# Gathered features per block from 16, 16, 16, 16 to 16, 15, 15, 15, with another way of comparing ids in the first block

## Chip, cores and metric

The kernel runs on one core of a Trainium2 chip. The metric is the device time of one execution in microseconds (us), the median of the runs shown; less is better.

## What is computed

A recommendation tower: for each of 2,048 samples 26 table rows are looked up by id, the 27 vectors (dense features and 26 rows) are multiplied with each other, and the 351 products go through three dense layers together with the dense features.

```
e = jnp.stack([tbl_0[ids[:, 0]], ..., tbl_25[ids[:, 25]]], axis=1)     # [2048, 26, 128]
combined = jnp.concatenate([dense_features[:, None, :], e], axis=1)    # [2048, 27, 128]
interactions = jnp.einsum('bfd,bgd->bfg', combined, combined)
z = jnp.concatenate([dense_features, interactions[:, _IU0, _IU1]], axis=1)   # upper triangle, 351
h = jnp.concatenate([z, dense_features], axis=1)                        # 607 columns
h = jnp.maximum(h @ W_top1 + b_top1, 0.0)      # 607 x 512
h = jnp.maximum(h @ W_top2 + b_top2, 0.0)      # 512 x 256
y = h @ W_top3                                  # 256 x 1
```

Four tables have 12,500 or 125,000 rows, the others 1,000 or 1,250.

## The kernel before

The samples are cut into 16 tiles of 128, four tiles to a block of 512. A table row reaches its sample in one of two ways.

- **Gathered** (`gather`, L676 to L682, on GpSimd's queue): per tile and feature one indirect DMA brings 128 rows to `rows`, which has room for two tiles. TensorE transposes them (`turn_group`, L806) in four groups of four features into PSUM; VectorE copies the even groups to `all_combined` (L1044), ScalarE the odd ones (L916).
- **Looked up** (`look_up`, L727): for a whole block and one feature TensorE multiplies the table, in chunks of 125 rows, with a one-hot matrix of 125 x 512 per chunk. A table of 1,000 rows has 8 chunks, one of 1,250 has 10. Each table is split in a high part (ScalarE's cast, L852) and a low part (VectorE's subtraction, "split", L1019), so each chunk is two matmuls. The one-hot matrices are made in halves of a look-up (4 or 5 chunks): by VectorE with one compare of ids against `row_bank`, row numbers that lie in PSUM (L1031), or, for the second half of the look-ups in `ACT_HOTS`, by ScalarE in two passes (L863, L870). `one_hot` holds 20 chunks. ScalarE copies the result out of PSUM (`copy_look`, L878) and later moves the looked-up columns of a tile to `all_combined` (`move_looks`, L897).

In every block the first 16 features of `SLOT_FEATURES` are gathered and the other 10 looked up. The looked-up features run forwards in even blocks and backwards in odd ones, so that a block's first four look-ups find their tables still in SBUF (`AGAIN`).

Per tile, TensorE multiplies the 27 vectors of four samples at a time (`dot_tile`, L821, four PSUM banks per tile, "dots"), ScalarE copies the banks (L925), and SP stores them to DRAM and loads them back as rows of pairs. The layers (L757, L766, L771, L783) of a block run during the next block ("products"); those of the last block run at the end in three pieces, with the exact fp32 product instead of three partial ones.

The order on TensorE is written out: the start (`START`) has all look-ups of block 0, with tile 0's transposes after the fourth; then per tile `dot_tile(t)` and `STEPS[t]`: the transposes of tile t+1, then `HALVES_AFTER` halves of look-ups for the next block, merged with products of the block before. VectorE keeps four halves ahead of it.

GpSimd's gathers for tile t+2 are let go in four steps:

```
pool.wait_ge(turned_done, groups_by(t))
gather(t + ROW_TILES, range(1))
for g in range(1, n_groups(t + ROW_TILES) - 1):
    if 0 < t <= LAST * PER_BLOCK:
        pool.wait_ge(half_done, halves_beside(t, g))
    gather(t + ROW_TILES, range(g, g + 1))
pool.wait_ge(dots_done, (t + 1) * FILLS - 1)
gather(t + ROW_TILES, range(n_groups(t + ROW_TILES) - 1, n_groups(t + ROW_TILES)))
```

So the last group of tile t+2 waits for the third bank of tile t's dots. SP's queue loads ids (`load_ids`, one row spread over all partitions, `ID_PLACES` look-ups of them), tables, weights, and carries the products' way through DRAM.

## Time and profile before

| what | value |
|---|---|
| timed runs, median (lowest to highest) | 379.48 us (379.36 to 380.45) |
| profiled execution, span (its own time is given as this span) | 496.1 us |
| PE, DVE, ACT, POOL busy in the span | 76%, 49%, 39%, 51% |
| instructions in the profile | 8,109 |
| DMA moved | 58.44 MB |

Engines: PE is TensorE (PEld its weight loads), DVE VectorE, ACT ScalarE, POOL GpSimd, SP the engine that issues most DMAs. A matmul in full fp32 leaves two records, one in fp32r leaves one: 64 matmuls of a tile's dots are 128 records. "issue" after a row means that the engine stood idle before it and waited for nothing that the profile shows; "remote" is a releaser that the profile does not know. The profiled execution is 116.6 us longer than the median of the timed ones.

### The profile page before, as it was taken

What the parts mean: (1) busy time and instruction counts of PE and PEld (TensorE: products, weight loads), DVE (VectorE), ACT (ScalarE), POOL (GpSimd) and SP (SyncE); (2) the same over time, 40 slices, a digit from 0 to 9 for tenths busy, and PEclk for the clock granted to TensorE, in tenths of its full rate; (3) what the DMA queues carried; (4) which work ended last, traced back from release to release, by engine and by line L of the source; (5) the groups of instructions that cost most, each with busy time, mean ns of one, the idle gap of its engine ahead of it and who ended that gap; (6) DMA issues with size and microseconds to landing.
All of it is one profiled execution on the core that took longest, in us unless ns stands there. A gap on an engine that the chain in (4) does not pass through costs nothing.

```text
span 496.1 us, 8109 instructions
## 1 busy us (share of the span) xinstructions
PE 376.0 (76%) x3360; PEld 301.4 (61%) x3360; DVE 244.4 (49%) x174; ACT 195.0 (39%) x261; POOL 254.8 (51%) x266
## 2 busy tenths in 40 slices
PE   1951777858586665978798796969788696879997
PEld 1630656647474554767586666867676455666787
DVE  4740789674919370765725750956566101112133
ACT  3810986414242521525252532434354334344400
POOL 6774540655737363646666554747466564730000
PEclk9985799989989796989998898989899898789899
DMA  8841763259915153456714533536232621123330
GB/s 210 218 134 41 218 187 85 70 156 275 227 29 161 45 155 103 109 150 153 183 46 128 160 87 104 143 93 193 74 89 63 168 73 27 49 63 100 69 71 5
DMA packets 38479, 58.44 MB, mean 118 GB/s; under 512 B 21665, under 2 KB 22561, under 8 KB 38444
## 3 DMA queue, kind: packets, MB, share of 16 engines
q1 hardware_dynamic: 29304, 40.74, 30.3%
q0 software_dynamic: 8192, 16.79, 13.5%
q8 instruction: 26, 0.43, 0.4%
q10 hardware_dynamic: 948, 0.41, 0.4%
q14 instruction: 9, 0.07, 0.0%
HBM read 47.68 MB, written 10.23 MB: 117 GB/s over the span
## 4 chain that ended last, share of the span: by engine, by line
PE 58%; issue 16%; DVE 11%; another core or an unknown queue 8%; SPq 3%; DMA 2%; ACT 2%; DVEq 0%; ACTq 0%
PE look_bank L727 25%; PE short_bank L821 15%; DVE one_hot L1031 8%; PE out_bank L757 6%; PE out_bank L771 4%; PE short_bank L806 4%; PE out_bank L766 3%; SPq L632 2%; DVE all_combined L1044 1%; DVE low_table L1019 1%; DMA spread_ids<-in_ids_by_feature 1%; PE out_bank L783 1%; SPq L621 1%; DMA last_scratch<-all_dots 1%
## 5 line engine op out<-in xcount | busy, mean ns | idle before, releaser
L682 POOL DMA_INDIRECT rows<-in_tbl,all_ids x256 | 253.9, 992 | 191.9 <-PE short_bank L821 81.9
L1031 DVE TENSOR_TENSOR one_hot<-spread_ids,row_bank 128x2048 fp32r<-128x2048 int32 (+3 forms) x80 | 170.7, 2175 | 27.1 <-PE look_bank L727 10.7
L727 PE MATMUL look_bank<-one_hot,high_table 125*128 125x512 f32 x328 | 140.8, 429 | 20.0 <-issue 16.1
L727 PE MATMUL look_bank<-one_hot,low_table 125*128 125x512 f32 x328 | 132.4, 404 | 0.6 <-issue 0.6
L821 PE MATMUL short_bank<-all_combined 128*59 128x54 f32 x2048 | 88.1, 247 | 53.2 <-issue 51.5
L821 PEld LDWEIGHTS short_bank<-all_combined 128*59 128x59 f32 x2048 | 79.7, 162 | 66.7 <-issue 66.5
L1044 DVE COPY all_combined<-short_bank 128x512 f32<-128x512 f32 x32 | 21.8, 691 | 156.2 <-PE short_bank L806 122.3
L727 PEld LDWEIGHTS look_bank<-one_hot,high_table 125*128 125x128 f32 x328 | 64.5, 197 | 40.5 <-issue 23.6
L727 PEld LDWEIGHTS look_bank<-one_hot,low_table 125*128 125x128 f32 x328 | 64.6, 197 | 16.9 <-issue 4.1
L925 ACT COPY all_dots<-short_bank 128x432 f32<-128x432 f32 x64 | 33.1, 518 | 97.1 <-remote 53.7
L878 ACT COPY looked_up<-look_bank 128x512 f32<-128x512 f32 x40 | 23.4, 586 | 120.8 <-remote 45.3
L806 PE MATMUL short_bank<-identity,rows 128*128 128x128 f32 x256 | 40.0, 290 | 38.7 <-issue 22.5
L806 PEld LDWEIGHTS short_bank<-identity,rows 128*128 128x128 f32 x256 | 28.9, 146 | 47.0 <-issue 27.0
L1019 DVE TENSOR_TENSOR low_table<-whole_table,high_table 125x1024 fp32r<-125x1024 f32 (+1 forms) x28 | 34.8, 1243 | 33.5 <-ACT high_table L852 22.7
L897 ACT COPY all_combined<-looked_up 128x1280 f32<-128x1280 f32 (+2 forms) x20 | 39.7, 1985 | 0.2
L852 ACT CAST high_table<-whole_table 125x1024 fp32r<-125x1024 f32 (+1 forms) x28 | 29.7, 1065 | 7.7 <-DMA whole_table<-in_tbl 7.7
L771 PE MATMUL out_bank<-hidden,w 128*128 128x512 f32 (+2 forms) x96 | 32.4, 470 | 0.0
L938 ACT ACTIVATE hidden<-out_bank,bias 128x512 f32<-128x512 f32 x18 | 15.4, 858 | 33.2 <-PE out_bank L757 18.3
L916 ACT COPY all_combined<-short_bank 128x512 f32<-128x512 f32 x32 | 19.9, 674 | 8.4 <-PE short_bank L806 8.4
L771 PEld LDWEIGHTS out_bank<-hidden,w 128*128 128x128 f32 x96 | 16.8, 199 | 6.3 <-issue 4.3
L1053 DVE TENSOR_SCALAR hidden<-out_bank,bias 128x128 f32<-128x128 f32 (+1 forms) x18 | 7.9, 437 | 22.2 <-PE out_bank L766 17.9
L863 ACT ACTIVATE one_hot<-spread_ids,chunk_row 128x512 fp32r<-128x512 int32 x24 | 15.4, 714 | 0.0
(42 smaller groups left out, 183.5 us busy)
## 6 DMA issues: line engine op xcount, KB each, us to landing
whole_table<-in_tbl SPq DMA_DIRECT2D x26, 448.0 KB
spread_ids<-in_ids_by_feature SPq DMA_DIRECT2D x40, 256.0 KB
block_scratch<-all_dots SPq DMA_DIRECT2D x24, 208.0 KB
rows<-in_tbl,all_ids POOLq DMA_INDIRECT x256
block_scratch<-all_dots SPq DMA_DIRECT2D x24, 104.0 KB
pairs<-block_scratch SPq DMA_DIRECT2D x72, 29.2 KB
whole_table<-in_tbl SPq DMA_DIRECT2D x26, 52.0 KB
whole_table<-in_tbl SPq DMA_DIRECT2D x2, 560.0 KB
```

Of the source, the lines that this page charges most:

```text
L682: nc.gpsimd.indirect_dma_start(rows[:, t % ROW_TILES, slot, :], None, tables[SLOT_FEATURES[slot]][:, :], bass.IndirectOffsetOnAxis(ap=all_ ...
L727: last = nc.tensor.matmul(look_bank[s % LOOK_BANKS][:], table_parts[part][TABLE_PLACE[s]][0:ROWS_K, c, :], one_hot[0:ROWS_K, (chunks_befor ...
L757: last = nc.tensor.matmul(out, w1_parts[weight][0:rows_k, k, i * P:(i + 1) * P], of_parts[of], start=(k == 0 and weight == of), stop=(k == ...
L771: last = nc.tensor.matmul(out, w2[:, k, o * P:(o + 1) * P], hidden1[:, k, a:b], start=(k == 0), stop=(k == last_k))
L806: last = nc.tensor.transpose(turn_bank(t, g)[:, q * P:(q + 1) * P], rows[:, t % ROW_TILES, slot, :], identity[:])
L821: last = nc.tensor.matmul(fill_bank(t, b)[row:row + LOADED, q * SQUARE:(q + 1) * SQUARE], all_combined[:, at:at + LOADED], all_combined[:, ...
L852: nc.scalar.copy(high_table[i][0:ROWS_K, 0:c, :], whole_table[i][0:ROWS_K, 0:c, :]).then_inc(table_high, 1)
L897: nc.scalar.copy(combined[:, :, 1 + GATHERED[m] + slot:1 + GATHERED[m] + slot + b - a], looked_up[:, place:place + b - a, u * P:(u + 1) * ...
L925: nc.scalar.copy(dots_of(h)[:, :, at:at + PER_BANK], fill_bank(t, b)[:, 0:PER_BANK * SQUARE].rearrange("p (q c) -> p c q", q=PER_BANK)).th ...
L1019: nc.vector.tensor_tensor(low_table[i][0:ROWS_K, 0:c, :], whole_table[i][0:ROWS_K, 0:c, :], high_table[i][0:ROWS_K, 0:c, :], ALU.subtract) ...
L1031: last = nc.vector.tensor_tensor(one_hot[:, place:place + n, :], spread_ids[:, s % ID_PLACES:s % ID_PLACES + 1, :].to_broadcast([P, n, COLS]),
L1044: nc.vector.tensor_copy(to, of).then_inc(even_copied, 1)
```

## The change

Blocks 1 to 3 gather 15 features and look up 11; the added one is feature 21, whose table has 1,250 rows. Their last group of transposes has three features. The numbers of halves per tile become 6, 5, 5, 6. `looked_up` has 16 places for 15, with a general search for the block that used a place before; `spread_ids` has 6 for 7. In block 0 (`s < FIRST_LOOK[1]`) VectorE compares one chunk per instruction, with the row number as an operand per partition from `chunk_row` in SBUF; in later blocks it compares as before. ScalarE makes 4 halves of block 0 (look-ups 1, 3, 5, 7) where it made 6 (1, 2, 4, 5, 7, 8).

```diff
-GATHERED = [16, 16, 16, 16]
+GATHERED = [16, 15, 15, 15]
...
-ID_PLACES = 7
-LOOK_PLACES = 15
+ID_PLACES = 6
+LOOK_PLACES = 16
...
-GROUPS = [[4, 4, 4, 4] for _ in range(BLOCKS)]
+GROUPS = [[4] * (n // 4) + [n % 4] * (n % 4 > 0) for n in GATHERED]
...
-HALVES_AFTER = [[6, 5, 5, 4] for _ in range(LAST)]
+HALVES_AFTER = [[6, 5, 5, 6], [6, 5, 5, 6], [6, 5, 5, 6]]
...
-ACT_HOTS = [1, 2, 4, 5, 7, 8]
+ACT_HOTS = [1, 3, 5, 7]
...
-    return BLOCK_OF[s] % 2 * (LOOK_PLACES - IN_BLOCK[0]) + LOOK_SLOT[s]
+    return BLOCK_OF[s] % 2 * (LOOK_PLACES - IN_BLOCK[BLOCK_OF[s]]) + LOOK_SLOT[s]
+
+
+def block_before(s):
+
+    earlier = [BLOCK_OF[i] for i in range(s) if look_place(i) == look_place(s)]
+    return earlier[-1] if earlier else None
...
             def copy_look(s):
-                if s >= LOOK_PLACES:
-
-                    act.wait_ge(look_moved, moves_by(BLOCK_OF[s - LOOK_PLACES] * PER_BLOCK + PER_BLOCK - 1))
+                if block_before(s) is not None:
+
+                    act.wait_ge(look_moved, moves_by(block_before(s) * PER_BLOCK + PER_BLOCK - 1))
...
-                for c, n, place in runs_of(s, h):
+                if s < FIRST_LOOK[1]:
+
+                    for c in halves(s)[h]:
+                        last = nc.vector.tensor_scalar(
+                            one_hot[:, (chunks_before(s) + c) % HOT_PLACES, :], spread_ids[:, s % ID_PLACES, :],
+                            chunk_row[CHUNKS[s]][:, c:c + 1], None, ALU.is_equal)
+                for c, n, place in runs_of(s, h) if s >= FIRST_LOOK[1] else []:
```

VectorE in the start, from its first half on, before (names: output, then inputs; partitions x elements, and the number of equal instructions in a row):

```order
L1031 TENSOR_TENSOR one_hot<-spread_ids,row_bank 128x2048
L1019 TENSOR_TENSOR low_table<-whole_table,high_table 125x1024
L1031 TENSOR_TENSOR one_hot<-spread_ids,row_bank 128x2048 x2
L1019 TENSOR_TENSOR low_table<-whole_table,high_table 125x1024
L1031 TENSOR_TENSOR one_hot<-spread_ids,row_bank 128x2048
L1019 TENSOR_TENSOR low_table<-whole_table,high_table 125x1024
L1031 TENSOR_TENSOR one_hot<-spread_ids,row_bank 128x2048
L1019 TENSOR_TENSOR low_table<-whole_table,high_table 125x1024
```

and the same place in the changed kernel:

```order
L1039 TENSOR_SCALAR one_hot<-spread_ids,chunk_row 128x512 x4
L1025 TENSOR_TENSOR low_table<-whole_table,high_table 125x1024
L1039 TENSOR_SCALAR one_hot<-spread_ids,chunk_row 128x512 x8
L1025 TENSOR_TENSOR low_table<-whole_table,high_table 125x1024
L1039 TENSOR_SCALAR one_hot<-spread_ids,chunk_row 128x512 x4
L1025 TENSOR_TENSOR low_table<-whole_table,high_table 125x1024
L1039 TENSOR_SCALAR one_hot<-spread_ids,chunk_row 128x512 x8
L1025 TENSOR_TENSOR low_table<-whole_table,high_table 125x1024
```

Each 2,048-column compare became four of 512 columns; the second half of look-up 2 is VectorE's now (the second x8), that of look-up 3, later, ScalarE's.

VectorE after tile 3's dots, where the fourth stretch of a block is prepared, before:

```order
L1044 COPY all_combined<-short_bank 128x128x4 x2
L1031 TENSOR_TENSOR one_hot<-spread_ids,row_bank 128x2048 x4
L1044 COPY all_combined<-short_bank 128x128x4 x2
```

and in the changed kernel:

```order
L1056 COPY all_combined<-short_bank 128x128x4 x2
L1043 TENSOR_TENSOR one_hot<-spread_ids,row_bank 128x2560 x2
L1025 TENSOR_TENSOR low_table<-whole_table,high_table 125x1280
L1043 TENSOR_TENSOR one_hot<-spread_ids,row_bank 128x2560
L1043 TENSOR_TENSOR one_hot<-spread_ids,row_bank 128x512
L1043 TENSOR_TENSOR one_hot<-spread_ids,row_bank 128x2048 x3
L1056 COPY all_combined<-short_bank 128x128x4 x2
```

The halves made here are six for four, three of them belonging to the 10-chunk tables (five chunks each, cut at the end of the 20 places), with the added split between them.

## Rows read from the trace of the kernel before

**Rows 1.** The page, busy time, share of the span and instructions per engine.

```profile
PE 376.0 (76%) x3360; PEld 301.4 (61%) x3360; DVE 244.4 (49%) x174; ACT 195.0 (39%) x261; POOL 254.8 (51%) x266
```

**Rows 2.** Waits: engine, line, releaser: us in total, times, longest us.

```profile
POOL rows L682 <- PE short_bank L821: 81.9, 14, 19.0
POOL rows L682 <- issue: 68.3, 224, 0.3
...
PE short_bank L821 <- issue: 51.5, 60, 2.0
...
PE short_bank L806 <- issue: 22.5, 20, 2.4
...
PE look_bank L727 <- issue: 16.7, 7, 10.1
```

**Rows 3.** Timeline of TensorE and ScalarE, 24 to 49 us: start, us, instruction, [idle before].

```profile
24.27 0.40 PE L727 MATMUL look_bank<-one_hot,low_table 125*128 125x512 f32 x1
...
48.42 0.58 ACT L878 COPY looked_up<-look_bank 128x512 f32<-128x512 f32 x1 [21.65 <-remote]
```

**Rows 4.** Timeline of TensorE, the last tiles.

```profile
442.56 2.10 PE L806 MATMUL short_bank<-identity,rows 128*128 128x128 f32 x16
...
447.28 7.03 PE L771 MATMUL out_bank<-hidden,w 128*128 128x512 f32 x16
454.24 3.68 PE L821 MATMUL short_bank<-all_combined 128*59 128x54 f32 x128
...
459.22 1.84 PE L783 MATMUL out_bank<-w,hidden 128*128 128x1 f32 x16
...
466.27 3.68 PE L821 MATMUL short_bank<-all_combined 128*59 128x54 f32 x128 [0.79 <-issue]
```

**Rows 5.** Groups by line, the gathers: count, busy us, mean ns, idle before.

```profile
L682 POOL DMA_INDIRECT rows<-in_tbl,all_ids x256 | 253.9, 992 | 191.9 <-PE short_bank L821 81.9 <-issue 68.3 <-PE short_bank L806 27.8
```

**Rows 6.** Timeline of TensorE, first and last of 35 look-up matmuls in a row.

```profile
95.69 0.39 PE L727 MATMUL look_bank<-one_hot,low_table 125*128 125x512 f32 x1
...
103.40 0.39 PE L727 MATMUL look_bank<-one_hot,low_table 125*128 125x512 f32 x1
```

**Rows 7.** Groups by line and shape, VectorE and ScalarE.

```profile
L1031 DVE TENSOR_TENSOR one_hot<-spread_ids,row_bank 128x2048 fp32r<-128x2048 int32 x61 | 137.3, 2282 | 23.6 <-PE look_bank L727 10.7 <-remote 5.7 <-DMA spread_ids<-in_ids_by_feature 3.9
...
L1019 DVE TENSOR_TENSOR low_table<-whole_table,high_table 125x1024 fp32r<-125x1024 f32 x26 | 31.8, 1224 | 31.8 <-ACT high_table L852 22.7 <-issue 9.1
...
L897 ACT COPY all_combined<-looked_up 128x1280 f32<-128x1280 f32 x12 | 29.7, 2474 | 0.0
...
L878 ACT COPY looked_up<-look_bank 128x512 f32<-128x512 f32 x40 | 23.4, 586 | 120.8 <-remote 45.3 <-PE look_bank L727 40.7 <-issue 34.8
L1044 DVE COPY all_combined<-short_bank 128x512 f32<-128x512 f32 x32 | 21.8, 691 | 156.2 <-PE short_bank L806 122.3 <-issue 24.1 <-remote 9.8
...
L1031 DVE TENSOR_TENSOR one_hot<-spread_ids,row_bank 128x2560 fp32r<-128x2560 int32 x7 | 19.5, 2815 | 0.0
...
L1019 DVE TENSOR_TENSOR low_table<-whole_table,high_table 125x1280 fp32r<-125x1280 f32 x2 | 3.0, 1488 | 1.7 <-issue 1.7
L852 ACT CAST high_table<-whole_table 125x1280 fp32r<-125x1280 f32 x2 | 2.5, 1256 | 0.0
```

**Rows 8.** Timeline of VectorE, ScalarE and GpSimd in the start.

```profile
3.16 1.10 POOL L682 DMA_INDIRECT rows<-in_tbl,all_ids  x1 [1.63 <-DMA all_ids<-in_ids]
...
5.71 2.29 DVE L1031 TENSOR_TENSOR one_hot<-spread_ids,row_bank 128x2048 fp32r<-128x2048 int32 x1 [3.90 <-DMA spread_ids<-in_ids_by_feature]
...
11.97 2.56 ACT L863 ACTIVATE one_hot<-spread_ids,chunk_row 128x512 fp32r<-128x512 int32 x4
14.56 2.01 ACT L870 ACTIVATE one_hot<-one_hot,ones 128x2048 fp32r<-128x2048 f32 x1
...
51.12 1.28 DVE L1044 COPY all_combined<-short_bank 128x512 f32<-128x512 f32 x2
```

**Rows 9.** Timeline of VectorE in the last products, a tensor_scalar of 256 columns.

```profile
464.67 0.48 DVE L1053 TENSOR_SCALAR hidden<-out_bank,bias 128x256 f32<-128x256 f32 x1 [4.56 <-PE out_bank L766]
```

**Rows 10.** Timeline of TensorE, transposes of tile 3 with the gap before the third group.

```profile
144.25 0.66 PE L806 MATMUL short_bank<-identity,rows 128*128 128x128 f32 x4 [1.08 <-issue]
```

**Rows 11.** Timeline, two gathers beside splits on VectorE, with the splits.

```profile
14.36 1.22 DVE L1019 TENSOR_TENSOR low_table<-whole_table,high_table 125x1024 fp32r<-125x1024 f32 x1
...
14.91 1.48 POOL L682 DMA_INDIRECT rows<-in_tbl,all_ids  x1 [0.30 <-issue]
...
61.54 1.49 DVE L1019 TENSOR_TENSOR low_table<-whole_table,high_table 125x1280 fp32r<-125x1280 f32 x1 [1.70 <-issue]
...
61.99 1.86 POOL L682 DMA_INDIRECT rows<-in_tbl,all_ids  x1 [0.30 <-issue]
```

## The prediction

> **What bounds the kernel now.** Busy shares come first [rows 1]: TensorE leads, and GpSimd, which only issues row gathers, is far behind. Neither says which of them sets the time, because this profiled execution is not paced like the timed ones: its span is 496.1 us and the median of the timed runs is 379.48, 116.6 less. The waits say where that went [rows 2]: TensorE stood 51.5 + 22.5 + 16.7 = 90.7 us with nothing shown to wait for, nearly all of it inside dot products and transposes. Where this happens, signals come late too: a look-up whose last matmul went out at 24.27 is copied only at 48.42, by a ScalarE that stood 21.65 us [rows 3]. Undisturbed pieces of the same work exist: a tile's dots in 3.68 us and its 16 transposes in 2.10 [rows 4]. So I take durations from undisturbed pieces, rebuild the schedule, and apply the difference to the median.
>
> GpSimd: a gather lasts 0.992 us on average and is followed by 0.30 of issue (68.3 us over 224) [rows 2, 5], 1.292 each; 16 make 20.7 us per tile. Its long waits (81.9 us for dots) are waits for a TensorE that this execution slowed.
>
> TensorE, undisturbed, per tile: dots 3.68, transposes 2.1 with 0.2 of hand-over, together 6.0. A look-up matmul starts every 0.227 us (34 steps in 7.71) [rows 6], two per chunk, so 0.453 a chunk; 82 chunks a block are 37.2 us, 9.3 a tile. A unit of the dense layers is 48 of the same matmuls (10.9), 7.03 and 1.84 [rows 4], 19.8, 4.9 a tile. That gives 15.3 us per tile in block 0 (no layers yet), 20.2 in blocks 1 and 2, about 11 to 16 in block 3. Against 20.7 for gathers: **GpSimd is a little slower than TensorE in three blocks and much slower in the last.**
>
> The start: VectorE makes 14 halves in it (12 x 2.28 + 2 x 2.82 = 33.0), 10 splits (9 x 1.22 + 1.49 = 12.5) and two copies (1.3) [rows 7], from 5.7 us on [rows 8], and waits about 3 for ScalarE: its last half is ready at 55.5. The matmuls of two halves, a copy and a move follow: tile 0's dots at 61. By then the first 44 gathers are out (3.2 + 44 x 1.29 = 60).
>
> From there GpSimd alone: the last group of tile 2 is let go by tile 0's third bank of dots at 63.8, that of tile 15 is 13 x 20.7 later, 332.9; 8.5 us for four gathers, landing, transposes and copies give tile 15's dots at 341.4, and from those dots to the end the trace has 29.8 (466.27 to 496.1) [rows 4]: 371. TensorE alone would give 61 + 4 x 15.3 + 8 x 20.2 + 44 (three tiles of block 3) + 29.8 = 357. Passing the two from tile to tile does not change 371. The median is 8.3 above; this is spread over slower gathers, TensorE gaps I cannot see, and time outside the span. The rates differ so little that this remainder matters.
>
> **The change, part by part.**
>
> *Gathers.* 12 fewer (244 for 256): 15 x 1.292 = 19.4 us a tile from tile 4 on. GpSimd alone: 60 + 2 x 20.7 + 11 x 19.4 = 314.8 for tile 15's last group, end 353. Worth 12 x 1.292 = 15.5 us where gathers set the pace. The 12 transposes are worth 12 x 0.13 = 1.6.
>
> *Look-ups.* Each of blocks 1 to 3 gets an eleventh, of a 1,250-row table: 10 chunks x 0.453 = 4.5 us of TensorE, 13.6 in all. VectorE gets three times two 5-chunk halves (2 x 2.82) and a split (1.49), 7.1 a block. Its block then has about 69 us of work (51.7 of chunks, 9 of splits, 5.5 of copies, 2.4 of other subtractions) beside at least 66 of TensorE in block 0 and 85 in blocks 1 and 2; it runs four halves ahead, which covers the difference in block 0. ScalarE gets three copies (0.59), three casts (1.26) and longer moves (1,408 columns for 1,280 in 2.47: 0.25 more each), under its idle time. SP gets three more id loads and three tables; six id places keep six look-ups in hand, so I cost them at nothing; if that cover were gone, the next half would wait for an id row (3.9 us of such waiting at the start [rows 8]).
>
> *Where the look-ups go.* All four stretches of a block are full now (6, 5, 5, 6); the added work is in the fourth, where block 0 had TensorE slack: 16.4 us per tile against 19.4 of gathers. In blocks 1 and 2 it is 21.3 against 19.4: **the lead changes to TensorE.**
>
> *The start.* VectorE's 4-chunk compare becomes four compares of 512 columns with an SBUF operand per partition. No row shows that form. Above: a 512-column copy from PSUM, 0.69; below: half the columns at the 2,048-column rate, 0.28 (2.28 / 8) [rows 7]. I take 0.43, near the 256-column tensor_scalar (0.48, less an overlap of 0.05 as between two copies in a row, 1.28 for 2 x 0.69 less 0.10) [rows 7 to 9]: that is right if two columns pass per cycle. The Trainium skill ("VectorE: DVE Perf Modes", the errata section) gives 58 + FD/2 cycles for such an op with both ends in SBUF, which I estimate as 0.33 us; with it the start would be one or two us shorter. VectorE then has 16 halves, 66 x 0.43 = 28.4, for 14 in 33.0. ScalarE loses two halves at 4.57 (2.56 + 2.01) [rows 8]. Walked through again, with VectorE now waiting 5.7 for casts, the last half is ready at 53.3 and tile 0's dots start at 57: **4 us gained**. But GpSimd's 44 gathers still end at 60, so this comes through only where TensorE leads.
>
> *Sum.* TensorE alone: 57 + 4 x 16.4 + 8 x 21.3 + 43.4 + 29.8 = 366. This needs gathers undisturbed in the start. If the compares stretch them as splits do (0.5 us each [rows 11], ten times), the last group of tile 5 starts at 60 + 5 + 2 x 20.7 + 19.4 = 125.8 instead of 120.8, and that tile's dots (18.6 later: landing, transposes, look-ups, products) at 144.4 instead of TensorE's own 142.4: 2 us more, 368. Against 371, 3 to 5 less. If the 8.3 us are all slower gathers (8.3 / 208 of gathering more, 1.33 each), the change is about 7.6 less; if they are TensorE gaps or outside the span, 2 to 4 less. I take 4.5: **375 us**.
>
> **The rivals.**
>
> *Gathers bound it all the way* (chance 0.15). Then most of 15.5 comes back: 379.5 - 15.5 = 364. For: GpSimd alone is the larger sum before. Against: TensorE's own sum after is 366, above GpSimd's 353.
>
> *TensorE bound it already* (0.23). The price is the added look-ups less transposes, 13.6 - 1.6 = 12, less 0 to 4 of the start, plus what moves cost: 7.5 to 12, here 387 at the high end and 385 as its value. It decides if TensorE's true sum before is above about 372 instead of 357, that is if transposes really cost 3.8 a tile with their gaps (the gap of 1.08 between groups recurs in most tiles [rows 10]) and not 2.3. For: those gaps, TensorE's 76%. Against: tile 14 has 16 transposes in 2.10 with no gap [rows 4], and the copies they wait for were held back by late signals.
>
> *The new compares and the gathers block each other* (0.05). Rows: a gather beside a split, which reads two SBUF operands, took 1.48 and 1.86 in place of 0.94, while the split kept its time [rows 11]. So a neighbour stretches gathers; the compares could too, and 66 of them could each wait for a gather instead. Worked out: 44 x 0.94 of gathers and 28.4 of compares end to end, with 12.5 and 1.3, give 84 + 5.7 = 90 for the start, over 25 us late, some 400 us. The Trainium skill ("SBUF — State Buffer", on the shared port pair) says that a two-port VectorE operation and GpSimd exclude each other for a whole instruction; by that rule the time is this one. The trace agrees for gathers beside splits (1.48), and no run here shows the new form.
>
> *Gain and cost cancel* (0.12). Start not faster (compares at 0.56 or more), TensorE taking over earlier: 379 to 380.
>
> **How the numbers follow.** A measurement here separates about 0.3%, 1.1 us. Forecast 0.45 (370 to 378), gathers 0.15, cancel 0.12, TensorE already 0.23, blocking 0.05. Faster 0.45 + 0.15 = 0.60; same 0.12; slower 0.28. The range leaves out the blocked case, the lower half of the gathers case and a little of the slow one: 366 to 387.
>
> **What would show it.** Compares at 0.3 to 0.45 us on VectorE and tile 0's dots earlier; gathers beside them not above 1.5; GpSimd's waits for dots longer in blocks 1 and 2, since it now waits for TensorE; 716 look-up matmuls (656 + 60) at 0.227. Compares of 0.6 us, or gathers of 2 us beside them, would make the start term wrong. A time above 381 would mean that TensorE had no slack to give; one below 368 that gathers still lead.

## Result and the profile after

The changed kernel takes 391.43 us (median; 388.78 to 393.26), the kernel before in the same runs 379.9 us: ratio 1.0289, 95% interval 1.0247 to 1.0330. It is 11.5 us slower; 375 had been forecast, in a range that ended at 387.

The page of the changed kernel, answering to [rows 1]; its profiled execution took 393.26 us and is paced like the timed ones:

```profile
span 391.4 us, 8265 instructions
PE 350.6 (90%) x3408; PEld 287.5 (73%) x3408; DVE 258.8 (66%) x234; ACT 190.7 (49%) x257; POOL 260.3 (66%) x254
```

TensorE is busy 90% of the span. [Rows 1] had 76%, because that execution was disturbed; a second profile of the kernel before (first experiment) has 89%, so TensorE was as full before.

The groups by line of GpSimd and VectorE, answering to [rows 5, 7]; mean ns of one after the busy time:

```profile
L688 POOL DMA_INDIRECT rows<-in_tbl,all_ids x244 | 259.3, 1063 | 78.8 <-issue 72.2 <-PE short_bank L827 2.2 <-DMA all_ids<-in_ids 1.6
L1025 DVE TENSOR_TENSOR low_table<-whole_table,high_table 125x1024 fp32r<-125x1024 f32 x27 | 33.0, 1222 | 22.2 <-ACT high_table L858 21.9 <-issue 0.3
L1039 DVE TENSOR_SCALAR one_hot<-spread_ids,chunk_row 128x512 fp32r<-128x512 int32 x66 | 27.4, 481 | 6.8 <-DMA spread_ids<-in_ids_by_feature 4.2 <-PE look_bank L733 2.5
```

The compares are as cheap as expected: 481 ns on average for one, and in a row they overlap, 8 in 3.25 us (from 10.42 us on), 0.41 each; 512 more columns of the old form cost 0.53 (2.815 less 2.282, [rows 7]). The gathers are not: 12 fewer, but they keep GpSimd busier in sum than in [rows 5] (259.3 for 253.9; 263.5 in the undisturbed second profile). And GpSimd waits 2.2 us for dots where [rows 2] had 81.9, so the sign of a TensorE in the lead that the prediction named isn't there. But it was a poor sign. By the timelines, the last gather of tile 3 ends 19.4 us before that tile's dots and that of tile 12 ends 35.4 before its own: GpSimd starts late and catches up, hardly ever waiting, behind a TensorE that is slower than it from tile 4 on. In the kernel before it is the other way round: 22.1 us at tile 3, 15.6 at tile 12 and 4.5 at tile 15.

The timeline of GpSimd and VectorE in the changed kernel's start, where [rows 11] had 1.48 beside a split:

```profile
9.76 1.66 POOL L688 DMA_INDIRECT rows<-in_tbl,all_ids  x1 [0.30 <-issue]
11.72 1.28 POOL L688 DMA_INDIRECT rows<-in_tbl,all_ids  x1 [0.30 <-issue]
13.30 2.41 POOL L688 DMA_INDIRECT rows<-in_tbl,all_ids  x1 [0.30 <-issue]
...
17.51 0.94 POOL L688 DMA_INDIRECT rows<-in_tbl,all_ids  x1 [0.31 <-issue]
...
13.59 1.22 DVE L1025 TENSOR_TENSOR low_table<-whole_table,high_table 125x1024 fp32r<-125x1024 f32 x1
14.72 1.67 DVE L1039 TENSOR_SCALAR one_hot<-spread_ids,chunk_row 128x512 fp32r<-128x512 int32 x4
```

The gather of 13.30 lasts until the split and part of the four compares behind it are over; where VectorE is idle (17.51) a gather takes 0.94. Who waits for the late rows shows in TensorE's timeline, with the granted clock (third number from the end) of three stretches under it:

```profile
33.41 1.09 PE L812 MATMUL short_bank<-identity,rows 128*128 128x128 f32 x4 [3.09 <-DMA rows<-in_tbl,all_ids]
34.72 0.63 PE L733 MATMUL look_bank<-one_hot,low_table 125*128 125x512 f32 x1
...
105.05 1.09 PE L812 MATMUL short_bank<-identity,rows 128*128 128x128 f32 x4 [4.20 <-DMA rows<-in_tbl,all_ids]
34.00:36.00 2.00, 2.00 (x7) 1.62 (x6) 1.00 (x1) 2.00 (x2) 1.82 (x1) 0.50 0.20 59
94.00:98.00 4.00, 4.00 (x92) 3.41 (x92) 4.00 (x3) 2.15 (x4) 3.09 (x4) 1.00 0.88 211
104.00:108.00 4.00, 2.95 (x9) 2.56 (x10) 1.32 (x1) 0.67 (x1) 2.83 (x3) 0.62 0.37 112
```

Transposes of tile 0 and of tile 3 wait 3.09 and 4.20 us for rows. Behind either wait the granted clock is 0.50 for about 3 us, that is 1.2 GHz: a look-up matmul starts every 0.43 us and not every 0.227 (0.63 shown for 0.39). So a wait of 3 to 4 us costs some 1.5 more, an estimate from 3 us at half the rate; the pieces of other runs bear it out (under "Block 0" below).

The span in pieces, between the starts of the tiles' dot products as the timelines of TensorE give them (us). The kernel before is the undisturbed profile of the first experiment; the last three columns are experiments 2, 3 and 11:

| piece | before | changed | start only (2) | fifteens only (3) | splits halved (11) |
|---|---|---|---|---|---|
| start to dots of tile 0 | 60.7 | 61.4 | 65.8 | 60.3 | 61.5 |
| tiles 0 to 3 | 50.3 | 54.9 | 50.9 | 50.3 | 51.3 |
| 3 to 4 | 19.1 | 27.0 | 19.1 | 27.1 | 22.0 |
| 4 to 7 | 64.3 | 59.9 | 66.8 | 59.9 | 59.6 |
| 7 to 8 | 19.8 | 23.5 | 19.7 | 23.5 | 20.4 |
| 8 to 11 | 63.6 | 60.8 | 63.6 | 60.7 | 63.1 |
| 11 to 12 | 20.6 | 24.7 | 23.6 | 24.3 | 19.5 |
| 12 to 15 | 50.5 | 46.2 | 48.3 | 45.9 | 47.6 |
| 15 to the end | 29.8 | 33.0 | 29.8 | 31.4 | 29.8 |
| span | 378.7 | 391.4 | 387.6 | 383.4 | 374.8 |

Of the 12.7 us between the first two, 0.7 lie in the start, 4.6 in tiles 0 to 3 (the wait of 4.20 and the slow clock after it), 7.9 + 3.7 + 4.1 in the three fourth stretches with the added look-up, and 3.2 in the tail; the stretches between give back 4.4 + 2.8 + 4.3.

### The profile page after: what moved, and what is told of

The parts are those of the page before. It is cut to its first block, busy times and chain, and to the rows that moved or that the text cites. A ratio compares the mean times of both kernels' runs of the same rounds, so it can differ in the third digit from the quotient of the medians.

```text
span 391.4 us, 8265 instructions
## 1 busy us (share of the span) xinstructions
PE 350.6 (90%) x3408; PEld 287.5 (73%) x3408; DVE 258.8 (66%) x234; ACT 190.7 (49%) x257; POOL 260.3 (66%) x254
## 3 DMA queue, kind: packets, MB, share of 16 engines
q0 software_dynamic: 7808, 16.01, 15.3%
## 4 chain that ended last, share of the span: by engine, by line
PE 50%; POOL 19%; SPq 9%; issue 8%; DMA 6%; DVE 4%; ACT 2%; ACTq 1%
PE look_bank L733 23%; POOL rows L688 19%; PE short_bank L827 9%; PE out_bank L763 8%; SPq L638 7%; PE short_bank L812 4%; PE out_bank L777 3%; DMA rows<-in_tbl,all_ids 2%; SPq L627 2%; DMA last_scratch<-all_dots 2%; DVE one_hot L1043 2%; PE out_bank L772 1%; ACTq L1017 1%; PE out_bank L789 1%; DMA dense_cols<-in_r_dense_features 1%
## 5 line engine op out<-in xcount | busy, mean ns | idle before, releaser
L688 POOL DMA_INDIRECT rows<-in_tbl,all_ids x244 | 259.3, 1063 | 78.8 <-issue 72.2
L1043 DVE TENSOR_TENSOR one_hot<-spread_ids,row_bank 128x2048 fp32r<-128x2048 int32 (+3 forms) x71 | 154.4, 2219 | 16.3 <-PE look_bank L733 16.1
L733 PE MATMUL look_bank<-one_hot,high_table 125*128 125x512 f32 x358 | 150.4, 420 | 14.6 <-DVE low_table L1025 10.6
L733 PE MATMUL look_bank<-one_hot,low_table 125*128 125x512 f32 x358 | 143.1, 400 | 0.0
L827 PEld LDWEIGHTS short_bank<-all_combined 128*59 128x59 f32 x2048 | 57.4, 133 | 12.6 <-issue 11.1
L827 PE MATMUL short_bank<-all_combined 128*59 128x54 f32 x2048 | 59.8, 218 | 5.3 <-ACT all_combined L903 3.0
L1025 DVE TENSOR_TENSOR low_table<-whole_table,high_table 125x1024 fp32r<-125x1024 f32 (+1 forms) x31 | 38.9, 1256 | 24.0 <-ACT high_table L858 23.6
L931 ACT COPY all_dots<-short_bank 128x432 f32<-128x432 f32 x64 | 32.8, 520 | 26.6 <-PE short_bank L827 22.2
L812 PE MATMUL short_bank<-identity,rows 128*128 128x128 f32 x244 | 33.9, 286 | 12.3 <-DMA rows<-in_tbl,all_ids 7.3
L903 ACT COPY all_combined<-looked_up 128x1408 f32<-128x1408 f32 (+4 forms) x20 | 42.6, 2128 | 0.2
L1039 DVE TENSOR_SCALAR one_hot<-spread_ids,chunk_row 128x512 fp32r<-128x512 int32 x66 | 27.4, 481 | 6.8 <-DMA spread_ids<-in_ids_by_feature 4.2
L944 ACT ACTIVATE hidden<-out_bank,bias 128x512 f32<-128x512 f32 x18 | 15.6, 864 | 28.0 <-PE out_bank L763 22.2
L1065 DVE TENSOR_SCALAR hidden<-out_bank,bias 128x128 f32<-128x128 f32 (+1 forms) x18 | 7.9, 437 | 22.2 <-PE out_bank L772 17.8
L922 ACT COPY all_combined<-short_bank 128x512 f32<-128x512 f32 (+1 forms) x32 | 18.4, 627 | 7.4 <-PE short_bank L812 7.4
```

Of the source, the lines that this page charges most:

```text
L688: nc.gpsimd.indirect_dma_start(rows[:, t % ROW_TILES, slot, :], None, tables[SLOT_FEATURES[slot]][:, :], bass.IndirectOffsetOnAxis(ap=all_ ...
L733: last = nc.tensor.matmul(look_bank[s % LOOK_BANKS][:], table_parts[part][TABLE_PLACE[s]][0:ROWS_K, c, :], one_hot[0:ROWS_K, (chunks_befor ...
L812: last = nc.tensor.transpose(turn_bank(t, g)[:, q * P:(q + 1) * P], rows[:, t % ROW_TILES, slot, :], identity[:])
L827: last = nc.tensor.matmul(fill_bank(t, b)[row:row + LOADED, q * SQUARE:(q + 1) * SQUARE], all_combined[:, at:at + LOADED], all_combined[:, ...
L903: nc.scalar.copy(combined[:, :, 1 + GATHERED[m] + slot:1 + GATHERED[m] + slot + b - a], looked_up[:, place:place + b - a, u * P:(u + 1) * ...
L931: nc.scalar.copy(dots_of(h)[:, :, at:at + PER_BANK], fill_bank(t, b)[:, 0:PER_BANK * SQUARE].rearrange("p (q c) -> p c q", q=PER_BANK)).th ...
```

## The experiments

All ratios are to the kernel before, run on the same chip beside them, with 95% intervals.

**1. The kernel before, looked at again.** No edit.

> The kernel before, unchanged, for one more profile, since the first one was stretched to 496.1 us. Every theory expects 379 to 381 us. If the stretching was the profile's and not the kernel's, the span is now near 378 us, the idle time of TensorE with nothing shown to wait for falls from 90.7 us to under 25, and tile 0's dots start near 61 us (I had worked that out). If GpSimd set the pace before, its waits for dots fall from 81.9 us to under 15; if TensorE did, they stay above 25.

Measured: 381.25 us, span 378.7. Of its page and waits:

```profile
PE 335.5 (89%) x3360; PEld 274.1 (72%) x3360; DVE 243.3 (64%) x174; ACT 193.1 (51%) x261; POOL 264.5 (70%) x266
L682 POOL DMA_INDIRECT rows<-in_tbl,all_ids x256 | 263.5, 1029 | 79.3 <-issue 75.6 <-DMA all_ids<-in_ids 1.6 <-PE look_bank L727 1.2
PE short_bank L806 <- DVE all_combined L1044: 7.6, 6, 3.1
PE short_bank L806 <- DMA rows<-in_tbl,all_ids: 6.4, 4, 2.5
```

GpSimd hardly waits for anything but its own issue here, from its first gather to its last, which ends 4.5 us before tile 15's dots. So the gathers lead before the change, as the sum had it; one takes 1.33 us with its issue (1.029 + 0.30), not 1.292. TensorE waits 6.4 us for rows, all of it after tile 4's dots, and 7.6 for VectorE's copies of turned columns, 5.6 of it in block 0. The disturbed execution had not shown either.

**2 and 3. Either half of the change alone.** In 2, the compares and the four halves, with 16 gathered features everywhere. In 3, 16, 15, 15, 15 with the start of before.

```diff
 # 2
-ACT_HOTS = [1, 2, 4, 5, 7, 8]
+ACT_HOTS = [1, 3, 5, 7]
+                if s < FIRST_LOOK[1]:
...
+                        last = nc.vector.tensor_scalar(
...
+                            chunk_row[CHUNKS[s]][:, c:c + 1], None, ALU.is_equal)
 # 3
-GATHERED = [16, 16, 16, 16]
+GATHERED = [16, 15, 15, 15]
-HALVES_AFTER = [[6, 5, 5, 4] for _ in range(LAST)]
+HALVES_AFTER = [[6, 5, 5, 6], [6, 5, 5, 6], [6, 5, 5, 6]]
```

> The kernel before with only the start of the change: one-chunk compares with a row number per partition in block 0, and ScalarE's four halves 1, 3, 5, 7; 16 gathers and 10 look-ups in every block. Theory G (the compares stretch the gathers, and late gathers set the time): GpSimd has some 10 gathers fewer out at 61 us than at 1.29 us each, a delay of 8 to 12 us that nothing takes back: 386 to 391 us, most of the added 11.5. Theory L (the added look-ups cost the time): the start gains or loses little, 377 to 382 us.

> The changed kernel with the start of before: compares against row numbers in PSUM for all blocks and ScalarE's six halves; 16, 15, 15, 15 gathers stay, and so do six id places. Theory G: gathers in the start take 0.94 to 1.0 us again, TensorE has slack for part of the look-ups: 378 to 383 us. Theory L: 13.6 us of TensorE's look-ups less 1.6 of transposes, and VectorE's 7 us a block, come on top of a TensorE that was full: 388 to 393 us.

Measured: 2 is 390.75 us, ratio 1.0265 (1.0184 to 1.0346); 3 is 386.11, ratio 1.0151 (1.0059 to 1.0244). 3 lies between its two expectations (378 to 383, 388 to 393). Either half loses, 10 and 5.6 us, and together (11.5) they lose less than the sum: what the late gathers of 2 cost in tiles 4 to 15 (2.5 + 3.0 - 2.2 in the table) is not paid with 15. In 2, TensorE's longest wait for rows is longer than in the changed kernel:

```profile
36.58 1.09 PE L806 MATMUL short_bank<-identity,rows 128*128 128x128 f32 x4 [6.80 <-DMA rows<-in_tbl,all_ids]
```

**4. Fifteen in the last block only.**

```diff
+GATHERED = [16, 16, 16, 15]
+HALVES_AFTER = [[6, 5, 5, 4], [6, 5, 5, 4], [6, 5, 5, 6]]
```

> As the kernel before in its start, with 16, 16, 16, 15 gathers: the eleventh look-up is made in block 2 for block 3 only, and only tiles 12 to 15 gather 15 rows (halves 6, 5, 5, 4 in blocks 0 and 1, then 6, 5, 5, 6). Theory G: GpSimd leads most in the last tiles, four gathers less are 5.2 us, the look-up costs 4.5 where TensorE has little slack: 376 to 380 us. Theory L: 4.5 less 0.5: 383 to 385 us.

Measured: 380.33 us, ratio 1.0007 (0.9966 to 1.0048), just above the range of theory G. The added look-up lengthens the gap from tile 11 to 12 (24.3 for 20.6) and four gathers less take it back in tiles 12 to 15 (46.0 for 50.5): no difference. So in the last block the exchange is even, and what 3 loses comes from the first two exchanges, the one in block 0 above all (8.0 us, of which tiles 4 to 7 return 4.4).

**5 and 6. The start taken apart.** 5 is the compares alone, with ScalarE's six halves; 6 is four halves alone, with the compares of before.

```diff
 # 6
-ACT_HOTS = [1, 2, 4, 5, 7, 8]
+ACT_HOTS = [1, 3, 5, 7]
```

> The kernel before with one thing changed: in the first block VectorE compares chunk by chunk with a row number per partition (tensor_scalar). ScalarE keeps its six halves. Theory G (a tensor_scalar of 0.4 us holds back the gather that starts beside it, so fewer gathers are out when the start ends, and the late gathers set the time): 56 compares instead of 66, so gathers before 60 us cost some 6 us more in sum than in the kernel before (14.7 was seen with 66 compares, 6.2 without); 38 to 40 instead of 42 gathers are out when tile 0's dots start, that start is itself 2 to 4 us earlier (14 halves at 1.8 for 2.4), and the end is 4 to 7 us late: ratio 1.010 to 1.019. Theory L (VectorE, not the gathers, set what the start cost: its two extra halves are the price): the compares are cheaper here and no half is added, so the time falls by 2 to 4 us: ratio 0.990 to 0.996.

> The kernel before with one thing changed: ScalarE makes four halves of the first block's start instead of six, VectorE two more, with its own multi-chunk compares against the row numbers in PSUM. Theory G: gathers beside these compares keep 0.94 us, so 42 or more gathers are out when tile 0's dots start; VectorE has 2 x 2.3 to 2.8 us more, so tile 0's dots come up to 5 us late (60.7 to 63 to 66), but GpSimd goes on meanwhile and takes the next group only when the dots free its rows: the end is 0 to 4 us late: ratio 1.000 to 1.010. Theory L: VectorE's extra halves are what made the start cost 10 us: ratio 1.015 or more.

**7. Both operands in SBUF, in the old form.** The compares keep their multi-chunk form and their time, but read the row numbers from SBUF.

```diff
-                        bank_row(CHUNKS[s])[:, c:c + n].unsqueeze(2).to_broadcast([P, n, COLS]), ALU.is_equal)
+                        row_at(s)[:, c:c + n].unsqueeze(2).to_broadcast([P, n, COLS]), ALU.is_equal)
```

Here `row_at(s)` is `chunk_row[CHUNKS[s]]` in the first block and `bank_row(CHUNKS[s])` after it.

> The kernel before with one thing changed: in the first block the same multi-chunk tensor_tensor compares read the row numbers from SBUF instead of PSUM, so that both operands are in SBUF. This separates two reasons for slow gathers beside the new compares. If any second operand in SBUF is enough (as splits beside gathers, 1.5 to 1.9 us, suggest), the gathers beside these compares go to 1.3 to 2.4 us, their sum above 0.944 before 60 us rises from 6.2 to 15 or more, and the ratio is 1.01 to 1.03. If it is the two columns per cycle of the tensor_scalar alone, the gathers keep 0.94, the compares their 2.3 to 2.4 us, and the time is that of before: ratio 0.996 to 1.004.

Measured: 5 is 387.77 us, ratio 1.0179 (1.0093 to 1.0264). 6 is 379.87, ratio 0.9974 (0.9939 to 1.0010), a little better than either theory had it. 7 is 395.38, ratio 1.0397 (1.0325 to 1.0469), the slowest of all and beyond the 1.03 expected. The gathers that start between 3 and 60 us, in 1, 5, 6 and 7, groups by line:

```profile
L682 POOL DMA_INDIRECT rows<-in_tbl,all_ids x41 | 44.9, 1095 | 13.8 <-issue 12.2 <-DMA all_ids<-in_ids 1.6
L682 POOL DMA_INDIRECT rows<-in_tbl,all_ids x36 | 46.0, 1278 | 12.2 <-issue 10.7 <-DMA all_ids<-in_ids 1.6
L682 POOL DMA_INDIRECT rows<-in_tbl,all_ids x42 | 44.9, 1070 | 14.1 <-issue 12.5 <-DMA all_ids<-in_ids 1.6
L682 POOL DMA_INDIRECT rows<-in_tbl,all_ids x29 | 49.0, 1691 | 10.2 <-issue 8.5 <-DMA all_ids<-in_ids 1.6
```

and the compares and gathers of 7:

```profile
10.43 3.03 POOL L682 DMA_INDIRECT rows<-in_tbl,all_ids  x1 [0.30 <-issue]
...
10.36 4.48 DVE L1034 TENSOR_TENSOR one_hot<-spread_ids,chunk_row 128x2048 fp32r<-128x2048 int32 x2
L1034 DVE TENSOR_TENSOR one_hot<-spread_ids,chunk_row 128x2048 fp32r<-128x2048 int32 x10 | 22.7, 2284 | 4.0 <-DMA spread_ids<-in_ids_by_feature 4.0
```

The compares of 7 take 2284 ns, as before (2282), and only the place of one small operand differs; yet 12 gathers fewer are out by 60 us, and one beside a pair of them takes 3.03 us. So at equal length the memory that this form reads decides. Four halves by ScalarE cost nothing: the extra VectorE work lies beside gathers that go on undisturbed. In 1, the 120 gathers that start while a compare with its operand in PSUM runs all take 0.96 us or less. Between them, 5, 6 and 7 contradict the theory that the amount of VectorE's work set the price of the start: less of it cost 7.3 us (5), more of it nothing (6), and the same 15 us (7).

The Trainium skill ("SBUF — State Buffer", on the shared port pair) says that a VectorE operation in a two-port mode, or one with two SBUF inputs against a GpSimd operation that reads SBUF, excludes GpSimd for the whole instruction. The trace agrees: the gather of 10.43 ends 0.82 us after the first of the two compares beside it and takes 3.03 us for 0.94.

**8. The halves spread 6, 5, 6, 5.** Experiment 3 with one more half in the third stretch and one less in the fourth.

```diff
-HALVES_AFTER = [[6, 5, 5, 6], [6, 5, 5, 6], [6, 5, 5, 6]]
+HALVES_AFTER = [[6, 5, 6, 5], [6, 5, 6, 5], [6, 5, 6, 5]]
```

> 16, 15, 15, 15 gathered features with the start of the kernel before, as e3_fifteen_only, but VectorE makes 6, 5, 6, 5 halves in the four stretches of a block instead of 6, 5, 5, 6. In e3 the gap between the dots of tiles 3 and 4 was 27.1 us (19.1 before) and those after tiles 7 and 11 3.7 us more each than before. If the added look-up in the fourth stretch costs more than its own 4.5 us because VectorE comes to it with its copies and splits (3.4 us of waits in the first block), moving a half ahead brings the gap after tile 3 down by 2 to 3 us and the time by 2 to 4: ratio to before 1.005 to 1.010 where e3 had 1.0151. If all that counts is the sum of TensorE's work, the time stays within 1 us of e3: ratio 1.013 to 1.018.

Measured: 388.17 us, ratio 1.0172 (1.0081 to 1.0263), within its interval the time of 3. The gap from tile 3 to 4 shrinks (22.2 for 27.1), that from 2 to 3 grows (19.8 for 16.6): the work moves, the sum stays. Its runs came out as 385.4, 385.8, 390.5 and 390.7. The profiled one is of the upper pair, and shows what lifted it, in the same start as in 3: a wait of 3.15 us (1.24 there) and then the clock of the stretch 56 to 58 us.

```profile
55.76 0.79 PE L733 MATMUL look_bank<-one_hot,high_table 125*128 125x512 f32 x1 [3.15 <-ACT one_hot L876]
56.00:58.00 2.00, 2.00 (x5) 1.57 (x6) 2.00 (x2) 1.97 (x2) 1.70 (x2) 0.50 0.64 118
```

ScalarE had itself waited 1.21 us for a table before that half; two more microseconds of waiting on TensorE became five at tile 0's dots (65.7 for 60.3).

**9. The row number from PSUM.** As 5, the scalar operand read from PSUM.

```diff
-                            chunk_row[CHUNKS[s]][:, c:c + 1], None, ALU.is_equal)
+                            bank_row(CHUNKS[s])[:, c:c + 1], None, ALU.is_equal)
```

> The one-chunk tensor_scalar compares of the scalar start (ScalarE with its six halves), with the row number per partition read from the row numbers in PSUM instead of SBUF. The wide input and the output stay in SBUF. Theory G1 (what holds back a gather is a VectorE instruction with two operands read from SBUF, as splits and the tensor_tensor compares with rows in SBUF have them; here the row number is the second): the gathers keep 0.94 us beside these compares, 42 or more are out at tile 0's dots, ratio 0.990 to 1.000. Theory G2 (two columns per cycle, 0.41 us for 512, takes the second port by itself, whatever the scalar is): 36 gathers are out at tile 0's dots, the ratio is that of the run with the row number in SBUF, 1.0179, within 0.006. If the compare becomes slower than 0.41 us, that is the third case: the form loses the two columns per cycle with the PSUM operand.

Measured: 384.19 us, ratio 1.0116 (1.0069 to 1.0162). The compares keep their 0.41 us, and the gathers are held all the same:

```profile
L682 POOL DMA_INDIRECT rows<-in_tbl,all_ids x37 | 45.9, 1239 | 12.5 <-issue 11.0 <-DMA all_ids<-in_ids 1.6
L1033 DVE TENSOR_SCALAR one_hot<-spread_ids,row_bank 128x512 fp32r<-128x512 int32 x58 | 24.6, 489 | 6.8 <-DMA spread_ids<-in_ids_by_feature 4.3 <-PE look_bank L727 2.5
```

37 gathers by 60 us, against 36 in 5 and 41 in 1 (at tile 0's dots, where the expectation had counted them, 40, 36 and 42): it is the one-chunk form, not the row number's place, that holds GpSimd in the changed kernel. Which property of the form does it, its speed or that short instructions follow each other without a pause, no run separates. That its time lies 3.6 us under 5's is not explained; the intervals overlap.

**10. The changed kernel with only the compares' form undone.**

```diff
-                if s < FIRST_LOOK[1]:
+                if False:
...
-                for c, n, place in runs_of(s, h) if s >= FIRST_LOOK[1] else []:
+                for c, n, place in runs_of(s, h):
```

> The changed kernel with the form of the compares alone undone: 16, 15, 15, 15 gathered features, four halves by ScalarE, but multi-chunk tensor_tensor compares with the row numbers in PSUM. Theory G (the form costs, the count of ScalarE's halves does not): the time is that of the fifteens alone, ratio 1.015 (1.011 to 1.019), 41 or 42 gathers out at tile 0's dots, no gather over 2 us in the start. Theory L (VectorE's extra halves and look-ups are what costs, and add up with the fifteens): 1.025 or more, near the changed kernel's 1.0289.

Measured: 386.92 us, ratio 1.0168 (1.0125 to 1.0211), 44 gathers out at tile 0's dots. The form of 66 compares is worth 4.5 us of the changed kernel's 11.5, and the rest is the fifteens (3: 1.0151).

**11. Each split in two instructions**, on top of 6: a try for a faster kernel, with the 16s.

```diff
-                nc.vector.tensor_tensor(low_table[i][0:ROWS_K, 0:c, :], whole_table[i][0:ROWS_K, 0:c, :],
-                                        high_table[i][0:ROWS_K, 0:c, :], ALU.subtract).then_inc(table_split, 1)
+                for a, b in ((0, c // 2), (c // 2, c)):
+                    last = nc.vector.tensor_tensor(low_table[i][0:ROWS_K, a:b, :], whole_table[i][0:ROWS_K, a:b, :],
+                                                   high_table[i][0:ROWS_K, a:b, :], ALU.subtract)
+                last.then_inc(table_split, 1)
```

> The kernel before with four halves by ScalarE, and each split of a table (high from whole, both in SBUF) written as two instructions of half the columns. Splits beside gathers cost GpSimd 14.5 us in all before (22 gathers stretched by 0.66 on average). If a gather gets in between two instructions (one of 3.03 us beside a pair of 2.28-us compares ended inside the second), the stretch per gather falls by 0.2 to 0.4 and the gathers' sum by 4 to 8 us; GpSimd sets the time of the middle blocks, so the time falls: ratio 0.985 to 0.995. If a gather needs more than one turn, each instruction is waited for again and nothing is gained: 0.996 to 1.003, VectorE having 2 us more in sum under its idle time.

Measured: 375.84 us, ratio 0.9860 (0.9817 to 0.9903): **1.4% faster than the kernel before**, and more than the four halves alone give (6). Its gathers up to 60 us, and all of them:

```profile
L682 POOL DMA_INDIRECT rows<-in_tbl,all_ids x44 | 42.8, 972 | 14.7 <-issue 13.1 <-DMA all_ids<-in_ids 1.6
L682 POOL DMA_INDIRECT rows<-in_tbl,all_ids x256 | 251.2, 981 | 84.5 <-issue 77.4
```

How a split holds a gather, in the kernel before (1), two whole splits and the gathers beside them, and under these one halved split (11):

```profile
9.48 1.23 DVE L1019 TENSOR_TENSOR low_table<-whole_table,high_table 125x1024 fp32r<-125x1024 f32 x1 [0.88 <-ACT high_table L852]
9.55 1.97 POOL L682 DMA_INDIRECT rows<-in_tbl,all_ids  x1 [0.30 <-issue]
...
45.25 0.94 POOL L682 DMA_INDIRECT rows<-in_tbl,all_ids  x1 [0.30 <-issue]
45.28 1.23 DVE L1019 TENSOR_TENSOR low_table<-whole_table,high_table 125x1024 fp32r<-125x1024 f32 x1
...
9.20 1.29 DVE L1020 TENSOR_TENSOR low_table<-whole_table,high_table 125x512 fp32r<-125x512 f32 x2 [1.07 <-ACT high_table L852]
9.51 1.20 POOL L682 DMA_INDIRECT rows<-in_tbl,all_ids  x1 [0.30 <-issue]
```

The gather of 9.55 starts while the split runs and ends 0.81 us after it; that of 45.25 starts 0.03 before its split and isn't held at all, nor is the split. Of the starts and durations in 1, all 33 gathers that begin while such a subtraction runs end 0.81 or 0.82 us after it, and the 21 that begin just before one take 0.95 or less. So what a gather waits for is the end of the one instruction that runs at its start. In 11 the first half ends at 9.89, and the gather of 9.51 ends 0.82 after that, at 10.71, although the second half still runs: a shorter instruction holds a gather less. GpSimd's sum is 12.3 us less than in 1, and 3.9 to 4.9 us of that reach the end.

**12 and 13. Halved splits in the changed kernel, and with the fifteens alone (10).** The edit is that of 11.

> The changed kernel with one thing more: each split of a table in two instructions of half the columns, as in the fastest run so far (before with four halves and halved splits, 0.986). Theory S (the one-chunk compares cost little by themselves; what holds gathers is a split of 1.22 us, and the scalar start puts compares and splits back to back so that more gathers meet one): gathers beside halved splits stay near 0.95, the sum above 0.944 falls from 29 to about 12 us, 41 or more are out at tile 0's dots, and what is left of the change is the fifteens: ratio 1.008 to 1.018. Theory T (the compares of two columns per cycle exclude the gathers by themselves): the first 60 us still have 8 us or more of stretching, 37 to 38 gathers out at tile 0's dots, ratio 1.020 or more.

> 16, 15, 15, 15 gathered features with four halves by ScalarE, the compares of before, and each split in two instructions. Against before with the same start and halved splits (0.986). Theory TB (with 16 gathers the gathers set the pace, with 15 TensorE does, so halving the splits helps only the sixteens): this run gains little over the fifteens without it (1.0168): ratio 1.010 to 1.017. Theory LB (the gathers set the pace with 15 as well, and their stretching is the cost): it gains as much as the sixteens did, 0.011 to 0.013: ratio 1.000 to 1.006.

Measured: 12 is 389.35 us, ratio 1.0213 (1.0155 to 1.0271); 13 is 387.34, ratio 1.0156 (1.0103 to 1.0209), taken without its slowest run of 391.86. The gathers up to 60 us in 12 and its longest one, with VectorE beside it:

```profile
L688 POOL DMA_INDIRECT rows<-in_tbl,all_ids x36 | 46.4, 1289 | 12.3 <-issue 10.7 <-DMA all_ids<-in_ids 1.6
13.28 3.27 POOL L688 DMA_INDIRECT rows<-in_tbl,all_ids  x1 [0.30 <-issue]
...
13.56 1.29 DVE L1026 TENSOR_TENSOR low_table<-whole_table,high_table 125x512 fp32r<-125x512 f32 x2
14.76 1.67 DVE L1041 TENSOR_SCALAR one_hot<-spread_ids,chunk_row 128x512 fp32r<-128x512 int32 x4
```

Between compares of the new form, halving the splits brings no more gathers out by 60 us: 36, as in the changed kernel, and one held from 13.28 to 16.55, through the halved split and all four compares. The time is 0.7% below the changed kernel's, within the intervals. So the compares hold gathers by themselves. A gather that starts under the last compare of a row ends 0.8 us after it, as with a split (that of 16.02 in the changed kernel takes 1.18), but inside a row it is held longer than to the end of the first. How a gather gets its turn between short instructions isn't settled: it did between the halves of a split in 11, and did not here. And 13 is no faster than 10: with 15 gathers per tile, better gathers no longer help, so TensorE sets the pace there; with 16 the same edit gave over 1%.

## Why the prediction was wrong

The table of pieces stands against the sum "57 + 4 x 16.4 + 8 x 21.3 + 43.4 + 29.8 = 366":

| term | forecast | measured | difference |
|---|---|---|---|
| dots of tile 0 | 57 | 61.4 | +4.4 |
| block 0, four tiles | 65.6 | 81.9 | +16.3 |
| blocks 1 and 2, eight tiles | 170.4 | 168.9 | -1.5 |
| three tiles of block 3 | 43.4 | 46.2 | +2.8 |
| tile 15's dots to the end | 29.8 | 33.0 | +3.2 |

**Block 0 is the step that failed**: "where block 0 had TensorE slack", and with it VectorE's part, put at nothing because "it runs four halves ahead, which covers the difference in block 0". The 15.3 us per tile were a bare sum of TensorE's work. The second look at the kernel before has 69.4 us for the four tiles, 17.35 each. Block 0 in that execution (length; busy time of PE, PEld, DVE, ACT, POOL; granted clock), and TensorE's largest wait in it:

```profile
60.70:130.10 69.40, 60.75 (x740) 51.47 (x741) 63.54 (x40) 36.19 (x51) 53.55 (x53) 1.00 0.75 195
PE short_bank L806 <- DVE all_combined L1044: 5.6, 3, 3.1
```

TensorE's own work was summed rightly, 61.2 us for 60.75 measured. But VectorE has more, 63.5 us, its copies of turned columns come late, and TensorE stands 8.6 us; none of that is a wait for rows. So the block was already longer than either engine's sum, and there was far less room for another look-up than I took. To this come, in the changed kernel, 4.6 us for tile 3's last gather and the clock behind it, and 7.9 in the fourth stretch, of which 4.5 is the look-up. The other 3.4 have two parts. One is the clock: in this stretch TensorE waits 3 us for VectorE's copies in almost every run, and the clock falls behind that wait in some. The stretch in 1, 11 and the changed kernel (length, PE busy, granted clock):

```profile
111.00:130.10 19.10, 13.31 (x177) 1.00 0.52 135
112.80:134.80 22.00, 16.11 (x179) 0.84 0.52 131
116.30:143.30 27.00, 19.41 (x198) 0.94 0.56 143
```

With the same four halves it took 19.1 us at a mean clock of 1.00 (1, 2, 6), 20.1 to 20.7 at 0.92 (4, 5, 7, 9) and 22.0 at 0.84 (11). The changed kernel's 0.94 of 27 us is as much slow time as 0.92 of 20.7, so about 1.5 us of the 3.4, by estimate. The rest is the chain, as experiment 3 shows on VectorE: idle for places (3.48), two 5-chunk compares, and only then the split that TensorE waits for.

```profile
124.27 5.55 DVE L1043 TENSOR_TENSOR one_hot<-spread_ids,row_bank 128x2560 fp32r<-128x2560 int32 x2 [3.48 <-PE look_bank L733]
129.74 1.48 DVE L1025 TENSOR_TENSOR low_table<-whole_table,high_table 125x1280 fp32r<-125x1280 f32 x1
```

Experiment 8 says that moving these waits doesn't shorten the whole.

**The start.** "This needs gathers undisturbed in the start" was the right condition with too small a price: ten gathers stretched by 0.5 each, 5 us. Over 0.944 each, the 36 gathers before 60 us lasted 13.0 us longer in sum in the changed kernel, 6.2 before; at tile 0's dots 37 were out, not 44, and 42 in the kernel before. The compares' price (0.43 forecast, 0.41 measured) was right, but the 4 us gained did not come: tile 0's dots at 61.4 for 57. VectorE waited 9.1 us for ScalarE's casts, for 5.7 forecast, and 2.5 more for a place that TensorE freed late, behind the wait of 3.09 for tile 0's rows and its slow clock. The Trainium skill's figure ("VectorE: DVE Perf Modes", the errata section), from which I had estimated 0.33, is below the 0.41 here.

**The rival "the new compares and the gathers block each other"** had the mechanism, and by experiments 2 and 5 to 12 it is this one; its price of over 20 us was too high, because it put all compares and all gathers end to end, and the gathers were stretched by 13.0 us in sum instead, while the compares kept their 0.41: 10 us alone, some 4.5 with the fifteens. I gave it 0.05, on the ground of [rows 11], which showed gathers stretched and splits unchanged. These rows should have raised it: all of VectorE's compares in the start changed from an operand in PSUM to operands in SBUF alone.

**The rival "TensorE bound it already"** (385) has the other half: with 15 gathers TensorE led from tile 4 on (busy for 83.1 of the 83.4 us from there to tile 8's dots; the same 59.9, 23.5 and 60.8 us stand in 3, 10 and 12, whatever their start), and the added look-ups came through. What it missed is that gathers led before, and that 12 of them less returned 11.5 us (4.4 + 2.8 + 4.3) against the 15.7 (7.9 + 3.7 + 4.1) that the look-ups cost.

**The tail**, taken as 29.8 either way, grew to 33.0: a wait of 1.38 us for pairs of the last tiles, and behind it 3.5 us at a granted clock of 0.52 (381.5 to 385.0), where the kernel before has neither. SP's queue, which loads the pairs from scratch, in the changed kernel and, last, TensorE:

```profile
359.33 9.88 SPq L638 DMA_DIRECT2D pairs<-last_scratch  x12
369.26 1.87 SPq L627 DMA_DIRECT2D last_scratch<-all_dots  x4
372.43 4.69 SPq L638 DMA_DIRECT2D pairs<-last_scratch  x6
380.61 0.49 PE L772 MATMUL out_bank<-pairs,w 117*128 117x128 f32 x2 [1.38 <-DMA pairs<-last_scratch]
```

Why the pairs come later is not shown. In 10 the tiles 14 and 15 follow each other as fast (10.5 us) and the last of these loads goes out 18.6 us after tile 15's dots for 18.8 here, but TensorE doesn't wait and the tail is 30.2. No run relieved SP's queue.

**What held**: the median carried over to an undisturbed execution (378.7 of span for the 371 of the sum, the gap being mainly gathers of 1.33 us for 1.292), the rates of blocks 1 and 2, VectorE's prices, and six id places at no cost (no wait for id rows after the first).

## What to carry to other kernels

Before making a VectorE instruction cheaper beside GpSimd gathers, ask from which memory it reads and in which form: the slower compare with a PSUM operand left the gathers alone, two wide SBUF operands or the faster one-chunk form did not. Where one holds them, cutting it in two can pay, as with the splits here. Don't call the difference between two engines' bare sums slack; look for an undisturbed execution and compare the pace of the tiles themselves. Where two engines lead in turn, moving work from one to the other pays only as long as the receiver's own pace has room.

## Not expected of the hardware

- A gather's issue on GpSimd went from 0.94 us to as much as 3.06 (3.03 in the rows above) beside compares whose second operand had moved from PSUM to SBUF, at unchanged 2.28 us of VectorE (7); and a gather that starts under a split ends 0.82 after it, while one that starts 0.03 us before a split isn't held (1).
- After waits of TensorE of 3.09, 3.15 and 4.20 us the granted clock was 0.50 for 3 us or more (6 in experiment 8), though one wait of 3.09 us in the kernel before (until 120.7 us, for VectorE's copy) had no such stretch behind it, and the same wait of 2.9 to 3.1 us had one in 4, 5 and 9. In the changed kernel the mean over the span was 0.978, in the undisturbed one of before 0.991.
- The last gather of tile 3 was issued at 95.97 us and its rows landed 8.95 us later, by the chain of waits below, while tables and id rows filled the DMA engines (share 0.88 at 94 to 98 us, above).

```profile
95.97 8.95 DMA rows<-in_tbl,all_ids
105.05 1.09 PE short_bank L812 x4
```

- A profiled execution 116.6 us longer than the timed ones kept durations, but hid the pace and who waits for whom: GpSimd's 81.9 us of waits for dots are not there in the undisturbed one.
